# Where GpSimd's additions stand between its scatters and returns, and what TensorE runs around them: linear attention with a routed expert layer on one core

## The reference

```python
xn = layernorm(x)                                   # no gain, no bias
# attention: 16 heads of 8, feature map of 32
q, k, v = heads(xn @ w_qkv)
q_, k_  = exp(q @ proj - max), exp(k @ proj - max)  # per head, max over the 32
kv, k_sum = einsum('bhtf,bhtd->bhfd', k_, v), sum_t(k_)
att = (q_ @ kv) / (q_ @ k_sum + 1e-6)
y1 = att @ w_out + b_out
# experts: 8 of them, hidden 256, two for each token
scores = (xn @ router_w.T + router_b) / max(temperature, 0.1)
gates  = sinkhorn(scores, 3 rounds)     # rows over 8 experts, columns over 128 tokens
vals, idx = top_k(gates, 2);  share = vals / (sum(vals) + 1e-8)
y2 = xn + sum_k share_k * ((relu(xn @ wg[idx_k]) * (xn @ wp[idx_k])) @ wo[idx_k])
return x + y1 + y2
```

## Time and profile before

| | us |
|---|---|
| median of three runs | 319.39 (317.07 to 322.05) |
| the profiled execution, its time | 315.41 |
| the profiled execution, its span | 313.6 |
| TensorE busy | 280.3 |
| GpSimd busy | 233.9 |
| VectorE busy | 223.0 |
| ScalarE busy | 157.9 |

### The profile page before, as it was taken

One profiled execution on the slowest core, in us unless ns is written; L12 is line 12 of the kernel. 1 busy time (PEld: TensorE's weight loads), 2 busy tenths in 40 slices (PEclk: granted clock), 3 DMA queues, 4 the chain that ended last, 5 costly groups with the idle time before them and its releaser, 6 DMA issues.

```text
span 313.6 us, 6573 instructions
## 1 busy us (share of the span) xinstructions
PE 280.3 (89%) x2068; PEld 263.0 (84%) x2068; DVE 223.0 (71%) x522; ACT 157.9 (50%) x353; POOL 233.9 (75%) x357
## 2 busy tenths in 40 slices
PE   8997874999999999999999998999979999865950
PEld 7896864989999999999889997999979999745940
DVE  4969999558888888999856767777657774705056
ACT  2875403234444445554557767677766874312100
POOL 6999736878888888888026888888888888885600
PEclk9999987589999999999999999999999999975565
DMA  7975000921111111111425877888768831111974
GB/s 234 353 267 196 4 0 28 313 87 47 49 47 49 47 51 56 50 38 54 118 76 171 252 245 230 247 238 262 243 195 256 243 111 45 49 50 58 327 287 167
DMA packets 27469, 45.78 MB, mean 146 GB/s; under 512 B 5328, under 2 KB 16208, under 8 KB 27440
## 3 DMA queue, kind: packets, MB, share of 16 engines
q1 hardware_dynamic: 21312, 33.86, 34.4%
q0 software_dynamic: 4544, 9.84, 8.9%
q10 hardware_dynamic: 1584, 1.73, 1.6%
HBM read 27.73 MB, written 17.68 MB: 145 GB/s over the span
## 4 chain that ended last, share of the span: by engine, by line
PE 75%; DVE 13%; another core or an unknown queue 3%; issue 3%; DMA 3%; POOL 1%; ACT 1%; SPq 0%; DVEq 0%; ACTq 0%
PE bank L834 11%; PE bank L694 9%; PE bank L671 9%; PE bank L822 6%; PE bank L824 6%; PE bank L823 6%; PE bank L647 4%; PE bank L649 4%; PE bank L648 4%; PE bank L684 4%; PE bank L807 3%; PE bank L710 3%; PE bank L621 2%; PE bank L604 2%
## 5 line engine op out<-in xcount | busy, mean ns | idle before, releaser
L572 POOL DMA_INDIRECT rows_y<-xn,row_i x78 | 81.5, 1044 | 30.0 <-ACT xn L986 16.6
L910 ACT ACTIVATE feat<-z_sb 128x512 f32<-128x512 f32 x64 | 39.9, 631 | 71.5 <-DVE z_sb L1081 51.2
L545 POOL DMA_INDIRECT slots_x<-xn,slot_i x64 | 63.5, 992 | 10.9 <-issue 10.9
L1074 DVE TENSOR_REDUCE neg_max<-bank 128x16 f32<-128x512 f32 x64 | 42.7, 684 | 21.9 <-PE bank L649 10.4
L822 PE MATMUL bank<-xT_high,w_high 128*128 128x256 f32 x156 | 47.1, 302 | 3.4 <-issue 2.9
L824 PE MATMUL bank<-xT_high,w_low 128*128 128x256 f32 x156 | 44.0, 282 | 0.0
L823 PE MATMUL bank<-xT_low,w_high 128*128 128x256 f32 x156 | 43.9, 282 | 0.0
L1081 DVE TENSOR_TENSOR z_sb<-bank,neg_max 128x512 f32<-128x512 f32 x64 | 42.5, 683 | 0.5
L834 PE MATMUL bank<-w_tile,hidden 128*128 128x128 f32 x312 | 41.0, 275 | 0.0
L694 PE MATMUL bank<-kv_sb,qT_sb 128*128 128x36 f32 x256 | 33.5, 291 | 6.2 <-DVE kv_sb L1089 4.1
L694 PEld LDWEIGHTS bank<-kv_sb,qT_sb 128*128 128x128 f32 x256 | 33.1, 209 | 6.7 <-ACT qT_sb L921 4.3
(11 more groups left out here) (159 smaller groups left out, 554.3 us busy)
## 6 DMA issues: line engine op xcount, KB each, us to landing
w_tile<-w_expert_dram SPq DMA_DIRECT2D x39, 384.0 KB
slots_x<-w_tile SPq DMA_DIRECT2D x39, 144.0 KB, 2.2
x_tile<-slots_x SPq DMA_DIRECT2D x39, 144.0 KB
acc<-x_dram SPq DMA_DIRECT2D x8, 256.0 KB, 5.1
xn<-rows_y SPq DMA_DIRECT2D x8, 256.0 KB, 6.0
w_tile<-rows_y SPq DMA_DIRECT2D x8, 256.0 KB, 6.1
out_dram<-acc ACTq DMA_DIRECT2D x5, 256.0 KB, 2.0
rows_y<-xn,row_i POOLq DMA_INDIRECT x78
```

Of the source, the lines that this page charges most:

```text
L545: pool.indirect_dma_start(slots_x, bass.IndirectOffsetOnAxis(slot_i[k][:, i:i + 1], 0), xn[:, j, :], None).then_inc(scattered[n % FLIGHT], 16)
L572: pool.indirect_dma_start(rows_y, bass.IndirectOffsetOnAxis(row_i[:, k, t:t + 1], 0), y_tile(k, t), None)\
L910: act.activation(feat[par][n][:, :], z_sb[n][:, :], ACT.Exp).then_inc(feat_ready, 1)
L1074: dve.tensor_reduce(neg_max[n][:, :], args(n), AX_X, ALU.max, negate=True).then_inc(z_negmax, 1)
```

## The change

The pieces of xn that go with the scatters shrink to quarter tiles (32 columns) and cover tiles 16 to 31 only. Tiles 0 to 15 are added behind the last scatter, four tiles at a time (`add_xn_group`), and no longer before but after their projections. `fill_gap` stands behind every return: 64 pieces of bias, then 14 memsets. VectorE masks kv of batch 0 right behind the first pick of slots, picks the second choice's slots behind `z_shift(1)` of batch 0, and numbers the tiles in batch 1 instead of batch 0. TensorE runs nine filler products ahead of `counts()` and eight (before: seven, behind a wait) ahead of `qT(1)` of batch 0; ahead of the experts ten instead of two, then waits for all scatters and runs eight more.

```diff
+    BASE_PIECES = NT * 2 + NG // 2
...
+            def quarter_tile(n):
+                return NT // 2 + n // 4, slice(n % 4 * D // 4, (n % 4 + 1) * D // 4)
...
             def add_xn(n):
-                j, cols = half_tile(n)
+                j, cols = quarter_tile(n)
                 pool.tensor_tensor(acc[:, j, cols], acc[:, j, cols], xn[:, j, cols], ALU.add).then_inc(base_added, 1)
+            def add_xn_group(g):
+                pool.wait_ge(acc_added, (g + 1) * GROUP // 2)
+                tiles = acc[:, g * GROUP:(g + 1) * GROUP, :]
+                pool.tensor_tensor(tiles, tiles, xn[:, g * GROUP:(g + 1) * GROUP, 0:D], ALU.add).then_inc(base_added, 1)
...
-            CLOSE = 2 * SLOT_TILES - YR
-            def gaps_up_to(n):
-                return n if n < CLOSE else CLOSE + (n - CLOSE) // 2
-            GAPS = gaps_up_to(2 * SLOT_TILES)
             def fill_gap(n):
-                piece = n * 2 * NT // GAPS
-                if (n + 1) * 2 * NT // GAPS > piece:
-                    add_bias(piece)
+                if n < 2 * NT:
+                    add_bias(n)
                 else:
-                    pool.memset(spent[n - piece], 0.0)
+                    pool.memset(spent[n - 2 * NT], 0.0)
...
-                    if gaps_up_to(2 * k + t + 1) > gaps_up_to(2 * k + t):
-                        fill_gap(gaps_up_to(2 * k + t))
-            pool.wait_ge(base_added, 2 * NT)
+                    fill_gap(2 * k + t)
+            for g in range(NG // 2):
+                add_xn_group(g)
+            pool.wait_ge(base_added, BASE_PIECES)
...
                 if whole:
+                    pe.wait_ge(v_copied, NG)
+                    keep_warm(9, V_BANK)
                     counts()
                 if front:
                     z(2, f)
                 if whole:
                     z(3, f)
-                    pe.wait_ge(v_copied, NG)
-                    keep_warm(7, V_BANK)
+                    keep_warm(8, V_BANK)
...
             pe.wait_ge(acc_added, EARLY - 1)
-            keep_warm(2, 4)
+            keep_warm(10, 4)
+            for i in range(FLIGHT):
+                pe.wait_ge(scattered[i], 16 * NT * TOPK // FLIGHT)
+            keep_warm(8, 4)
             rows_T(0, 0, 0)
...
-            act.wait_ge(base_added, 2 * NT)
+            act.wait_ge(base_added, BASE_PIECES)
...
             def add_projection(b):
                 dve.wait_ge(proj_ready, b + 1)
-                dve.wait_ge(base_added, 4 * b + 4)
+                if late(b, NB // 2):
+                    dve.wait_ge(base_added, 8 * (b - NB // 2) + 8)
...
-                for k in range(TOPK):
-                    settle(dve.tensor_tensor(picked[k][:, :], chosen[k][:, :], position[:, :], ALU.mult))
-                    settle(dve.tensor_reduce(slot_f[k][:, :], by_tile(picked[k]), AX_X, ALU.add))
-                    dve.tensor_copy(slot_i[k][:, :], slot_f[k][:, :]).then_inc(slots_ready, 1)
+                pick_slots(0)
+            def pick_slots(k):
+                settle(dve.tensor_tensor(picked[k][:, :], chosen[k][:, :], position[:, :], ALU.mult))
+                settle(dve.tensor_reduce(slot_f[k][:, :], by_tile(picked[k]), AX_X, ALU.add))
+                dve.tensor_copy(slot_i[k][:, :], slot_f[k][:, :]).then_inc(slots_ready, 1)
...
+                if whole:
+                    mask_kv(b, par)
                 if front:
                     z_max(0, f)
                     z_max(1, f)
                     z_shift(0, f)
                     z_shift(1, f)
-                if isinstance(b, int) and b == 0:
+                if whole:
+                    pick_slots(1)
+                if isinstance(b, int) and b == 1:
                     number_tiles()
-                if back:
+                if back and not whole:
                     mask_kv(b, par)
```

More of the change, by code:

```diff
@@ L1231, in step @@
                 divides = tail and not (isinstance(b, int) and b == EARLY)
+                whole = isinstance(b, int) and b == 0
                 if divides:
```

## The result

The changed kernel takes 344.21 us (341.83 to 345.54), the kernel before 318.23 us (315.04 to 322.05), four executions each: a ratio of 1.0875 (95%: 1.0823 to 1.0927). It is 26 us slower, and the range given ended at 325.5. The profiled execution took 343.73 us for a span of 341.9.

A forecast was written before the change was run, and what follows sets the result against it. TensorE was taken as the bound: +3.5 (filler) - 0.7 (early start) - 1 (clock) = +1.8 us, all else hidden. The median of 319.39 shifted gives 321.2; 320.5 was taken, with a range of 312.5 to 325.5 us.

The forecast's parts named there:

- Bound: Whole kernel: TensorE bounds attention and experts; GpSimd has slack in the scatter stage, its returns 8 us in the tail.
- Scatter in pieces of 32 columns: Scatter stage: additions shortened to 269 ns save GpSimd 4.3 us, scatters end near 144; worth nothing to the total.
- Rival 1: Late attention: bare returns cause late TensorE results; operations behind them remove the passage, -5.0 to -1.6 us, 316.1; chance 0.27.
- Rival 2: Tail: late attention stays tied to the last return, so the end moves +3.3 to +4.3 us, 323.7; chance 0.17.
- Rival 4: Ahead of the experts: filler is off the path because most executions wait for rows there; 317.7 us; chance 0.07.
- Early mask: Batch 0: mask moved ahead of the second pick starts the second product near 52.9 instead of 53.65, 0.7 us gained.
- Start filler: Near the start: nine products fill the first hole, no clock fall at 45; second fall stays; 1 us gained.
- rival 3: After batch 0's second hole: clock is held or returns at once, 6 us gained instead of 1, 315.5; chance 0.07.
- the sum: TensorE's path: +3.5 for filler, -0.7 for early start, -1 for clock, +1.8 us in all; everything else hidden.
- Expert filler: Ahead of the experts: 32 more filler instructions of 0.11 us lie fully on TensorE's path, +3.5 us.
- Operations behind all returns: Return stage: eight more operations cost GpSimd 1.5 us; last return near 290.0, inside the 8 us of slack.
- Range: Whole kernel: 312.5 to 325.5 us, from rival 1 with more clock gain to rival 2 with 1.8 us to spare.

The follow-up runs named there:

- the filler's run: Kernel before with only the filler ahead of the experts changed (ten products, wait for all scatters, eight more, instead of two): 316.5 us against 313.0 on chip B, ratio 1.016.

## Why the prediction was wrong

**Bound.** Read rightly: TensorE alone until the experts. But the slack of GpSimd in the scatter stage was read as freedom to change its pace.

**Scatter in pieces of 32 columns: the step that failed.** "It is worth nothing: TensorE does not come for the rows before 155." The arithmetic held (an addition took 0.26 us, 0.269 was expected; the last scatter over at 143.8, expected 144; the group additions 1.25 us each, though the fourth waited 3.23 us for VectorE, with cover). What was never weighed is what the distance between two scatters does to TensorE: it costs 8.0% on chip A and 8.5% by the medians on D, and attention ends 28.0 us later in the profiled execution of the change. The material stood in the text. Rival 1 asked whether bare returns, some 1.4 us apart, make TensorE's results late, and then argued that in the scatter stage all is well "with an operation between any two". The condition is not an operation but a distance, and this part cut it by 0.07 us.

**Rival 1: its mechanism is borne out in part, and it stood at the wrong place.** On chip C an operation behind every return takes the late results out of the late attention, and then the returns and plane loads are the bound, as it said. In the changed kernel the two late batches take 7.85 and 10.0 us (291.88, 299.73, 309.72) instead of 17.5 at the worst, and on chip A about 12 remain: returns with memsets behind them are 1.47 us apart, so an operation between two is not enough everywhere. It forecast 1.0% less; the runs gave 3.2% less on chip A and, by medians alone, 1.4% on C. In the change this gain is a few us of the tail (-5.5) against 28.0.

**Rival 2** (late attention tied to the last return) did not happen: in the changed kernel VectorE adds the last projection at 317.46, before the last return (319.57). **Rival 4** is refuted by the chain of the filler's run.

**Early mask.** Expected at 52.9, found at 52.79. **Start filler.** The granted clock was 1.00 from 44 to 48.4, where it was 0.50 from 45, and fell in the stretch without work behind it (4.5 us expected, 48.4 to 52.79 found); the product after it took 3.63 us again, as forecast. The Trainium skill (TensorE: Matmul & The Clock Gate, part 1) has activity as what releases the clock; that the filler did it is not shown here. The fall near 45 is missing in all five profiles with the filler, but also in four of the eleven without it (those of the runs at 1.49, 1.59 and 1.26 us, and of all returns on chip A). In the same way the clock came back from the second fall between 59 and 69 us, early and late in kernels of either start. In the change it came back near 67.6, later than before (65.5), so rival 3 did not happen, and the 0.9 us gained at 52.79 are gone by the second product of batch 1 (67.86 against 67.33). Nothing of the 0.7 and the 1 us of the sum is left in this trace, and that the part as a whole is worth 1.7 us could not be measured (1.007, 0.999 to 1.015).

**Expert filler.** 36 instructions of 4.10 us, 4.0 expected, and +3.4 us on the path where the sum has +3.5. **Operations behind all returns.** First to last return +2.4 us, 1.5 expected; of the chain it matters only now that the returns are the bound.

**Range.** Its upper end came from the late attention and the returns, so it never covered the scatter stage, whose cost was taken as zero without a bound from above. The nearest row with closer DMAs (the late passage, 17.5 us for a batch instead of 7.85) would have given one.

**What stays open.** What in the chip holds TensorE's results back isn't settled: the runs show the dependence on the distance of GpSimd's indirect DMAs and nothing of the path. Fewer rows in one DMA at the same distance, or another number in flight than four, were not tried. Nor is it shown why chips differ: the unchanged kernel has medians of 336.26 and 340.65 us on two of them and 313.0 to 318.23 elsewhere. On A, the change with its scatters 1.51 us apart still has a granted clock of 0.74 from 120 to 140. On D, the kernel with two memsets keeps its whole attention up to 140 undisturbed and takes 334.11 us all the same, so the scatters are not all that is slower there.

## What to carry to other kernels

A cheap operation of GpSimd between two indirect DMAs can be a spacer that another engine's time hangs on; before it is shortened or moved, look at the distance of the DMAs and not at GpSimd's slack. Where a reader waits for "remote" after TensorE's record is over, look for indirect DMAs of GpSimd some 1.5 us apart or less, and space them with work that is needed anyway. Leave a margin, and measure on more than one chip: 1.51 us was enough, or nearly so, on chips B and C and not on A, and 1.58 to 1.66 us was enough on each of the three where it was tried. A cost that is put at nothing needs an upper bound as much as one that is counted.

## What the runs showed of the hardware

- The effect is steep: on chip A 0.07 us less between scatters (1.51 to 1.44) costs 8%, and 0.05 us given back (1.49) half of it. At 1.26 us, on chip B, TensorE's result reached VectorE 35.42 us after VectorE was ready for it (at 140.44; GpSimd issued scatters until 133.0).
- It isn't bandwidth: beside the slow batches the DMA engines are 14 to 15% busy at 49 to 53 GB/s, and in the kernel before, 14% busy at 50 GB/s from 80 to 120, TensorE never idles.
- Short waits are dear twice: of the 27.2 us of the six slow batches 15.1 are products at a lower granted clock, which falls to its lower level (1.2 GHz) behind idle stretches of 1.5 to 2.5 us that come once a batch.
- Kernels with the same start get their full clock back at different times: in the sixteen profiles the low stretch behind the second hole of batch 0 ends between 59 and 69 us.
